# Two samples' experts taken out of the place between the rounds and spread over the second round as a third stream

## What is computed

```python
x = x + tanh(g_xattn[0]) * cross_attention(layernorm(x), ctx)           # one head, 154 keys
x = x + tanh(g_ffn[0]) * two_layers(layernorm(x))                        # local attention, 8 heads, and a gated FFN
x = x + tanh(g_xattn[1]) * decoder_block(layernorm(x), ctx)              # diagonal self attention, 8-head cross attention, FFN
x = x + tanh(g_ffn[1]) * mixture_of_experts(layernorm(x))
# the last one, xf being the tokens:
probs = softmax(xf @ router_w + router_b)
tw, ti = top_k(probs, 8); tw = tw / sum(tw)
for e in range(64):                                                       # 64 routed experts, hidden width 32
    acc += cw[:, e] * (silu(xf @ w1[e] + b1[e]) @ w2[e] + b2[e])          # cw is tw where e is among ti, else 0
shared = sum over 2 of silu(xf @ sw1 + sb1) @ sw2 + sb2                   # 2 shared experts, hidden width 256
```

## Time and profile before

| | us |
|---|---|
| median of 3 runs | 1002.5 |
| lowest, highest | 1002.33, 1004.6 |
| the profiled execution | 1004.58 |
| its span | 1002.8 |

### The profile page before, as it was taken

One profiled execution on the slowest core, in us unless ns is written; L12 is line 12 of the kernel. 1 busy time (PEld: TensorE's weight loads), 2 busy tenths in 40 slices (PEclk: granted clock), 3 DMA queues, 4 the chain that ended last, 5 costly groups with the idle time before them and its releaser, 6 DMA issues.

```text
span 1002.8 us, 15716 instructions
## 1 busy us (share of the span) xinstructions
PE 742.8 (74%) x5368; PEld 489.7 (49%) x5368; DVE 562.2 (56%) x2206; ACT 498.7 (50%) x1315; POOL 297.2 (30%) x296
## 2 busy tenths in 40 slices
PE   5765487866786757699986686777757676768998
PEld 3444365544464635554444463555536455555543
DVE  5785455646654665635367555565555556464533
ACT  3436275574554545344544653755536354544443
POOL 3453314435232132130024242353333311331200
PEclk9877889888787888699998787798977988867999
DMA  8310010100100000042410101001010000002433
GB/s 288 111 38 1 11 39 1 48 2 11 38 2 11 1 1 2 14 126 77 142 37 1 37 7 42 1 11 38 1 47 2 11 1 2 1 1 61 114 97 96
DMA packets 35706, 39.47 MB, mean 39 GB/s; under 512 B 14169, under 2 KB 23467, under 8 KB 35499
## 3 DMA queue, kind: packets, MB, share of 16 engines
q1 hardware_dynamic: 35627, 38.47, 13.4%
HBM read 27.44 MB, written 1.57 MB: 29 GB/s over the span
## 4 chain that ended last, share of the span: by engine, by line
PE 46%; DVE 26%; ACT 17%; POOL 4%; issue 3%; DMA 1%; SPq 1%; DVEq 0%; POOLq 0%; ACTq 0%
ACT work L783 14%; PE act_psum L554 6%; PE moe_psum L564 5%; DVE work L1027 4%; PE dve_psum L421 4%; DVE work L1050 3%; PE dve_psum L390 3%; PE act_psum L634 3%; PE dve_psum L461 2%; PE dve_psum L637 2%; DVE res_nrm L1005 2%; DVE stats L996 2%; PE act_psum L451 2%; PE act_psum L527 2%; PE dve_psum L644 2%
## 5 line engine op out<-in xcount | busy, mean ns | idle before, releaser
L783 ACT ACTIVATE work<-work,nbias,rnorm 128x128 f32<-128x128 f32 x256 | 122.6, 480 | 75.1 <-DVE nbias L1087 75.0
L1384 POOL TENSOR_TENSOR work<-work,rinv 128x512 f32<-128x512 f32 (+1 forms) x80 | 84.7, 1076 | 249.7 <-DVE rinv L1014 249.7
L879 ACT ACTIVATE work<-act_psum,cols 128x512 f32<-128x512 f32 x80 | 54.6, 687 | 70.2 <-PE act_psum L554 70.2
L390 PE MATMUL dve_psum<-wqkv,hTs 128*128 128x512 f32 x128 | 72.3, 693 | 14.4 <-ACT hTs L905 13.8
L1366 POOL TENSOR_SCALAR rstd<-mv 128x4 f32<-128x4 f32 x36 | 10.1, 280 | 215.0 <-DVE mv L999 215.0
L1424 POOL TENSOR_TENSOR hT<-hT,work 128x512 f32<-128x512 f32 x32 | 40.6, 1270 | 108.5 <-DVE work L1050 108.4
L766 ACT COPY v_loc<-act_psum 77x512 f32<-77x512 f32 (+2 forms) x72 | 42.0, 583 | 61.3 <-PE act_psum L514 34.3
L1027 DVE CUSTOM_DVE_ANT_0 work<-dve_psum,masks 128x128 f32<-128x128 f32 x256 | 58.7, 285 | 23.2 <-PE dve_psum L421 23.2
L783 ACT ACTIVATE work<-work,nbias 128x154 f32<-128x154 f32 x128 | 52.3, 410 | 36.5 <-DVE nbias L1137 36.5
L766 ACT COPY hT<-act_psum 128x512 f32<-128x512 f32 (+1 forms) x60 | 31.0, 520 | 74.2 <-PE act_psum L451 35.4
L564 PE MATMUL moe_psum<-work,w_m 128*128 128x512 f32 x128 | 65.3, 598 | 1.0 <-DVE work L1193 1.0
(11 more groups left out here) (195 smaller groups left out, 1808.8 us busy)
## 6 DMA issues: line engine op xcount, KB each, us to landing
kT<-cwT_dram SPq DMA_DIRECT2D x160, 64.0 KB, 2.0
v_loc<-v_loc SPq DMA_DIRECT2D x24, 256.0 KB, 3.5
qT<-cwT_dram SPq DMA_DIRECT2D x96, 64.0 KB, 2.0
wqkv<-in_wqkv_dram SPq DMA_DIRECT2D x2, 768.0 KB
res_nrm<-in_x_dram SPq DMA_DIRECT2D x4, 256.0 KB, 2.9
w_m<-in_w_m_dram SPq DMA_DIRECT2D x1, 1024.0 KB, 9.1
v_loc<-v_loc SPq DMA_DIRECT2D x8, 128.0 KB, 3.1
shifted<-y SPq DMA_DIRECT2D x8, 128.0 KB
```

Of the source, the lines that this page charges most:

```text
L390: nc.tensor.matmul(bank[:], h, attn_w[:, k * INNER:(k + 1) * INNER], start=True, stop=True)\
L783: last = nc.scalar.activation(weights[:, i, :], weights[:, i, :], ACT.Exp, bias=nbias[u][:, b, i:i + 1], scale=scale_of(i), accum_out=sums ...
L879: nc.scalar.activation(dst, bank[:], ACT.Silu, bias=bias).then_inc(act_emptied, 1)
L1384: nc.gpsimd.tensor_tensor(some, some, by.unsqueeze(2).to_broadcast(list(some.shape)), ALU.mult).then_inc(ready[u], 1)
```

## The change

The experts of samples 0 and 1 (`is_deferred(u)`, u < 2) leave `sample_steps`: after the router these samples end at step 80, and slot 0 goes on to sample 2 at once, slot 1 to sample 3. A third generator, `deferred_experts(u)`, has 25 steps for each of them, with one chunk a step. `turns()` deals these 50 steps out evenly from the place where samples 2 and 3 begin to the end of their bodies, one for every 3.1 steps of the slots together.

The third stream has its own buffers: `experts_in` (the input `hT`, which goes to DRAM and comes back), `ahead` (two buffers for the experts' weights), `units` (three for the hidden units); x goes to DRAM as well and comes back at the end. To make room in SBUF, `shifted` becomes a view of the last row of `v_loc` (so the zeroing of its first token is done again in each layer, after the last `add_attention`), the four sums of rows are made in place, and `qs` and `ks` lie for a time in `kT[1]`. The banks of PSUM, the semaphores that count them, and the matmuls, activations and multiplications themselves are the same as before.

```diff
+DEFER = BATCH - len(SLOTS)
+DEFERRED_STEPS = 1 + CHUNKS + 2 + 2
+AHEAD = 2
...
+    total = ROUNDS * BODY_STEPS + EXPERT_STEPS
+    out, done, placed = [], [0, 0], 0
+    for slot in [0, 1] * TOGETHER + [0, 0, 1] * LEAD + [0, 1] * (total - TOGETHER - 2 * LEAD) + [1] * LEAD:
+        out.append(slot)
+        done[slot] += 1
+        begun = done[0] + done[1] - (2 * (BODY_STEPS + 1) - LEAD)
+        while placed < DEFER * DEFERRED_STEPS and placed * 2 * (BODY_STEPS - 2) < begun * DEFER * DEFERRED_STEPS:
+            out.append(len(SLOTS))
+            placed += 1
...
+                def deferred_experts(u):                      # PE
+                    yield
+                    pe.wait_ge(experts_in_loaded, 16 * (u + 1))
+                    for c in range(CHUNKS + 2):
+                        if c < CHUNKS:
+                            expert_hidden(u, c, experts_in)
+                        if c >= 2:
+                            expert_out(u, c - 2, units[(c - 2) % 3][:])
...
+                            nc.scalar.activation(units[c % 3][:], bank[:], ACT.Silu, bias=bias).then_inc(act_emptied, 1)
...
+                def deferred_experts(u):                      # DVE
+                    yield
+                    for c in range(CHUNKS + 2):
+                        k = c - 1 - SHARED
+                        if 0 <= k < ROUTED:
+                            rows_of, weights = units[(c - 1) % 3][:], ahead[k % AHEAD][:]
+                            dve.wait_ge(ahead_ready[k % AHEAD], ahead_fills(u, k))
+                            dve.wait_ge(act_emptied, act_item["moe_h", u, c - 1] + 1)
+                            nc.vector.tensor_tensor(rows_of, weights, rows_of, ALU.mult).then_inc(weighed_ready[u], 1)
+                        yield
...
+                    sp.dma_start(experts_in[:], hT_dram[u]).then_inc(experts_in_loaded, 16)
+                    sp.wait_ge(cwT_stored[u], 16)
...
+                            sp.wait_ge(weighed_ready[u], k + 1)
+                            if k + AHEAD < ROUTED:
+                                fill_ahead(k + AHEAD)
...
-                    if u + len(SLOTS) < BATCH:
+                    if is_deferred(u):
                         sp.wait_ge(ln_stats[u], LN_MOE + 1)
                         sp.wait_ge(act_emptied, act_item["hT_moe", u] + 1)
-                        load_sample(sp, u + len(SLOTS))
+                        load_sample(sp, u + DEFER)
+                        sp.dma_start(hT_dram[u], hT[u][:]).then_inc(hT_kept[u], 16)
+                        sp.dma_start(x_dram[u], flat(x[u])).then_inc(x_kept[u], 16)
```

More of the change, by code:

```diff
@@ L173, in build @@
         cols = sb("cols", [P, N_COLS])
-        rows = sb("rows", [P, N_ROWS])
+        rows = sb("rows", [P, KEPT_ROWS])
         ident = sb("ident", [P, P])
@@ L226, in build @@
         work = per_slot("work", [P, 3 * 2 * INNER])
+        shifted = [v[:, 2 * TILES - 1, :].rearrange("p (t d) -> p t d", t=TILES) for v in v_loc]
         ptb = [v[:, 2 * TILES - 2:, :].rearrange("p a n -> p (a n)").rearrange("p (h q) -> p h q", h=HEADS) for v in v_loc]
@@ L236, in build @@
         root = per_slot("root", [P, 2, 2 * HEADS])
+        experts_in = sb("experts_in", [P, SEQ])
+        ahead = [sb(f"ahead{j}", [P, SEQ]) for j in range(AHEAD)]
+        units = [sb(f"units{j}", [P, SEQ]) for j in range(3)]
         W2 = 2 * INNER
+        qk_scale = kT[1][:, 2, WINDOW:WINDOW + 4 * DH].rearrange("p (k l d) -> p k l d", k=2, l=LAYERS)
         rot_a, rot_b = (kT[1][:, k, WINDOW:].rearrange("p (t a d) -> p t a d", t=TILES, a=2) for k in range(2))
@@ L345, in all_samples, with in_turn @@
             act_item, dve_item = {}, {}
-            def in_turn(sample_steps):
+            def in_turn(sample_steps, deferred_experts):
                 steps = [chain.from_iterable(sample_steps(u) for u in SAMPLES[slot::len(SLOTS)]) for slot in SLOTS]
-                for slot in TURNS:
-                    next(steps[slot])
+                steps.append(chain.from_iterable(deferred_experts(u) for u in range(DEFER)))
+                for stream in TURNS:
+                    next(steps[stream])
                 assert all(next(step, "done") == "done" for step in steps)
@@ L563, in expert_out @@
                     w = w_s2[:, c, :] if c < SHARED else w_m2[:, c - SHARED, :]
-                    nc.tensor.matmul(moe_psum[:], w, weighed[u][:, c % 3, :], start=(c == 0), stop=False)
+                    nc.tensor.matmul(moe_psum[:], w, units_of, start=(c == 0), stop=False)
+                def deferred_experts(u):
[6 more added lines that the diff above has]
+                            expert_out(u, c - 2, units[(c - 2) % 3][:])
+                        if c == CHUNKS + 1:
+                            pe.wait_ge(ahead_ready[0], ahead_fills(u, ROUTED))
+                            nc.tensor.matmul(moe_psum[:], b_m2[:], ahead[0][0:EXPERTS, :], start=False, stop=True).then_inc(moe_filled, 1)
+                        yield
+                    pe.wait_ge(moe_emptied, u + 1)
+                    bank = dve_bank(("moe_out", u))
+                    for t in range(TILES):
+                        last = nc.tensor.transpose(bank[:, t * P:(t + 1) * P], units[2][:, t * P:(t + 1) * P], ident[:])
+                    last.then_inc(dve_filled, 1)
+                    yield
+                    yield
                 def sample_steps(u):
@@ L1187, in sums_of_rows, with deferred_experts @@
                     nc.vector.tensor_scalar(sb2_g[:], sb2_sum[:], gate[:, GF1:GF1 + 1], None, ALU.mult).then_inc(set_up, 1)
+                def deferred_experts(u):
+                    yield
+                    for c in range(CHUNKS + 2):
+                        k = c - 1 - SHARED
[4 more added lines that the diff above has]
+                            nc.vector.tensor_tensor(rows_of, weights, rows_of, ALU.mult).then_inc(weighed_ready[u], 1)
+                        yield
+                    bank = filled(("moe_out", u))
+                    dve.wait_ge(ahead_ready[1], ahead_fills(u, ROUTED))
+                    nc.vector.tensor_tensor(ahead[1][:], bank[:], ahead[1][:], ALU.add).then_inc(dve_emptied, 1)
+                    yield
+                    yield
                 def weigh(u, c):
```

160 lines of the change are left out of this document (114 added, 46 removed).

## The result

| | median us | runs | ratio to the kernel before, 95% interval |
|---|---|---|---|
| before | 1002.6 | 4 | |
| after | 972.3 (970.6 to 978.6) | 4 | 0.970 (0.966 to 0.974) |

The change takes 30.4 us away, where 10 were forecast. The direction and the range held, the size didn't: it is three times the forecast.

What follows compares the result with a forecast made beforehand. PE was taken to bound the expert stretches, the two samples' chains of waits the second round's bodies. Terms -54 + 30 + 18 + 6 - 10 = -10 us gave a predicted median of 992.5 us, range 956 to 1024 us.

Steps and rivals of the forecast that it cites:

- Part 1: From the end of sample 0's router to sample 3's first transposes: 40 us instead of 93.7, -54 us.
- Part 2: Expert matmuls inserted into the second round's bodies, 75 us at the mean clock, priced by PE's 40% chain share: +30 us.
- part 5: PE's granted clock in the second round rises from 0.83 to about 0.89 as matmuls are spread in: -10 us.
- Part 3: ACT in the second round's bodies: Silus and sums 25 us, 32 more table loads 41 us, of which +18 us lands.
- Part 4: DVE's 32 multiplications and two additions in the bodies, 23 us at 31%, with SP's queue counted in: +6 us.
- Rival B: ACT's table switches among exponentials of samples 2 and 3 take the gain back, slower: 1019.5 us with half on path; 30%.
- Rival A: Gaps in the second round's bodies swallow the third stream and the clock rises: -43 us, 960 us; 22%.

Runs made afterwards that it cites:

- The empty stream: The changed kernel with third-stream steps that hold no work, the experts of samples 0 and 1 left out: 951.8 us against 972.3 of the changed kernel.
- the pair on the empty stream: Third stream's 40 activations alone, without its matmuls, multiplications and broadcasts: 971.2 us as Silus with table loads, 955.8 us as Relu without loads.

## Why the forecast was off, point by point

- **Part 1, the stretch that goes** (-54, bounds -64 and -48): right. The empty stream gives -51.8; the stretch itself took 41.7 us there and 44.2 in the changed kernel, where 40 was taken.
- **Part 2, PE** (+30, less 10 for the clock in part 5, so +20): this is the step that failed. The matmuls alone cost 3.2 us. The price came from PE's share of the chain, 40% of 75 us. That share said rightly how much of the inserted work would lie on the chain (27 us, in the kernel with the matmuls alone), but not how far it would move the end: idle time took 31 us of it, the clock gave back 23, and the second stretch grew by 6. The lower price that was written down, 12 "if most fall into the 117 us of idle time", had the right reason; less the 10 for the clock it would have been 2. PE's busy share of the second stretch came out at 77%, where part 5 had nearly 85: it had set the inserted matmuls against a stretch that doesn't grow.
- **Part 5, the clock** (-10, mean 0.89): the clock was forecast right, 0.90 in the stretch, but its worth was taken from PE's part of the chain alone and it was kept apart from the insertion. What the runs show is the two together: matmuls in twos, spread over a stretch at 0.81, cost 3.2 us. Taking them as two separate terms, each by PE's share of the chain, left +20.
- **Part 3, ACT** (+18, bounds 8 and 50): right, 19.4 for the Silus with their loads. The share alone gave 13. By it the activations (25 us) would cost 5 and were measured at 4.0, the loads (41 us) 8 and were measured at 10.7 to 15.4. Raising the sum because loads stand among exponentials was right in direction; how much was a guess, and that it came within 2 us is in part luck. ACT's busy time in the stretch is 268 us where 270 was forecast. The drain that the Trainium skill (ScalarE: Activation LUTs, "What ACT_TABLE_LOAD costs") adds to a switch would, by the forecast's estimate, have made it 12 us later; the trace doesn't show one: 1.29 us after the load at 507.46 began, the Silu starts.
- **Part 4, DVE and SP** (+6): nothing that the runs show. The term was also added up a little low: 31% of 23 us are 7, and 1 for SP on top.
- With the measured terms the sum is -51.8 + 3.2 + 19.4 = -29.2 us; measured are -30.4.
- **Rival B** (ACT's switches make it slower) had the right mechanism for ACT: the switches are the larger part of what the third stream costs. From 16 us of ACT on the path it was to be slower, and 19.4 were on it; it is not, because PE's 31 us of that rival were 3. **Rival A** had PE's side nearly right (12 less 18 for the clock are -6, measured 3.2) and ACT's side wrong (10, measured 19.4); its 960 us are near what the whole stream comes to without the loads, 961.6.

## What to carry to other kernels

Independent work that is dealt out evenly in small pieces over a stretch that waits on dependencies can be nearly free on TensorE: here 69 us cost 3, with idle time filled and the granted clock up from 0.81 to 0.91. Price it by idle time plus what the clock gives back, and not by the engine's share of the chain, which says where work will lie and not what it costs. Don't count on the same for more of it: the next 69 us cost 24. The same stream is dear on the engine that has to change its function table for each piece (19.4 us, most of it loads). The pieces have to stay small and pipelined across steps: putting two together saved 11 table loads and lost the whole gain, by longer bursts and by waits for work of the same step.

## What was not expected of the hardware

- 60 us of matmuls added to a 392 us stretch (69 in the whole kernel) cost 3 us at the median (6 in the profiled stretch), with the granted clock going from 0.81 to 0.91; the next as many, in fours, cost 24.
- The same 80 matmuls in fours instead of twos cost 11 us more, though nothing waits for a result of theirs.
- 38 table loads fewer are worth 10.7 us in the full stream, 0.28 us each of their 1.28; by the pair on the empty stream 0.41 each.
